# Gated linear attention with a routed spline layer on one core: a new order of the four engines in the loop, and the product into the output issued in two parts

## What is computed

```python
shift = silu(causal_depthwise_conv(x, conv_w, conv_b))      # 4 taps
r, k = split(shift @ in_proj_w.T)                            # 64 + 64
u = sigmoid(x @ ch_gate_w0.T @ ch_gate_w1.T + ch_gate_b1) * x
mg = shift @ mem_gate_w.T + mem_gate_b
sel = softplus(mg[..., :M]); tau = sigmoid(mg[..., M:])
g = -sel * tau
k = k / maximum(norm(k), 1e-12) * sel ** tau
def step(S, inp):                                            # over the tokens
    S = exp(g_t)[..., None] * S + k_t[..., None] * u_t[:, None, :]
    o_t = SCALE * einsum('bm,bmd->bd', r_t, S)
x = layernorm(x + o + shift * residual_weight)
# routed layer: signs of the normed x against the tiles' signatures give a
# cluster and a tile in it; 16 features of the token go through that tile's
# splines, scaled by each tile's minimum and maximum over all tokens
x = layernorm(x + x + out)
```

## Time and profile before

| what | value |
|---|---|
| three runs, us | 1296.23, 1296.49, 1297.90 |
| median, us | 1296.49 |
| the profiled execution, us | 1294.74 |
| its span, us | 1293.0 |
| PE busy | 1154.4 us, 89% |
| DVE busy | 1091.9 us, 84% |
| ACT busy | 952.5 us, 74% |
| POOL busy | 830.0 us, 64% |
| HBM read, written | 69.06 MB, 101.01 MB |

### The profile page before, as it was taken

One profiled execution on the slowest core, in us unless ns is written; L12 is line 12 of the kernel. 1 busy time (PEld: TensorE's weight loads), 2 busy tenths in 40 slices (PEclk: granted clock), 3 DMA queues, 4 the chain that ended last, 5 costly groups with the idle time before them and its releaser, 6 DMA issues. The chain is left out here.

```text
span 1293.0 us, 31770 instructions
## 1 busy us (share of the span) xinstructions
PE 1154.4 (89%) x9346; PEld 733.4 (57%) x9346; DVE 1091.9 (84%) x2532; ACT 952.5 (74%) x1809; POOL 830.0 (64%) x1669
## 2 busy tenths in 40 slices
PE   5799999999999999999999999999999977469730
PEld 4556666666666666666666666666666643333100
DVE  4898888898999899989898999899989883686885
ACT  4657888888888888888888888888888754514781
POOL 3125666777767676767676767676767664524486
PEclk8999999999999999999999999999999987655555
DMA  4012222222222222222222222222222115769998
GB/s 143 33 38 103 104 104 105 104 103 103 103 103 103 103 103 103 103 103 103 103 103 103 103 103 103 103 103 103 103 103 103 71 71 201 264 244 342 376 415 323
DMA packets 63347, 174.86 MB, mean 135 GB/s; under 512 B 11195, under 2 KB 22339, under 8 KB 63302
## 3 DMA queue, kind: packets, MB, share of 16 engines
q1 hardware_dynamic: 52646, 151.43, 31.5%
q10 hardware_dynamic: 5280, 20.97, 4.1%
q0 software_dynamic: 5376, 1.91, 1.0%
HBM read 69.06 MB, written 101.01 MB: 132 GB/s over the span
## 5 line engine op out<-in xcount | busy, mean ns | idle before, releaser
L1052 DVE SCALAR_TENSOR_TENSOR acc<-xT_all,cw_sb,acc 128x256 f32<-128x256 f32 x768 | 353.8, 518 | 6.8 <-ACT acc L751 6.8
L777 ACT ACTIVATE sg<-TX,bet,gam 128x256 f16<-128x256 f32 x256 | 129.8, 557 | 39.9 <-issue 20.1
L1384 POOL TENSOR_TENSOR AT<-AT,Wm 128x128 f32<-128x128 f32 x224 | 114.9, 513 | 40.6 <-DVE AT L1078 24.8
L484 PE MATMUL PR<-xT_all,w_sb 128*128 128x256 f32 x512 | 136.4, 390 | 4.2 <-ACT xT_all L715 4.2
L496 PE MATMUL WK<-w_sb,tS 128*128 128x512 f32 x256 | 137.3, 618 | 0.0
L751 ACT ACTIVATE acc<-xT_all,cb_sb,cw_sb 128x256 f32<-128x256 f32 x256 | 132.5, 592 | 4.8 <-DVE xT_all L1038 2.8
L538 PE MATMUL OB<-th_all,AT 128*128 128x512 f32 x256 | 124.6, 609 | 12.3 <-POOL AT L1384 10.7
L566 PE MATMUL PR<-shT,w_mg_sb 128*64 128x128 f32 x2048 | 128.9, 280 | 6.4 <-ACT shT L760 6.4
L566 PE MATMUL PR<-shT,w_rk_sb 128*64 128x128 f32 x2048 | 125.9, 276 | 0.0
L566 PEld LDWEIGHTS PR<-shT,w_rk_sb 128*64 128x64 f32 x2048 | 110.5, 137 | 25.7 <-issue 25.7
L566 PEld LDWEIGHTS PR<-shT,w_mg_sb 128*64 128x64 f32 x2048 | 113.5, 139 | 18.8 <-issue 12.0
(11 more groups left out here) (236 smaller groups left out, 2698.4 us busy)
## 6 DMA issues: line engine op xcount, KB each, us to landing
xin_all<-in_x SPq DMA_DIRECT2D x32, 1024.0 KB
y_ring<-y_all SPq DMA_DIRECT2D x32, 1024.0 KB, 4.1
y_scratch<-y_all SPq DMA_DIRECT2D x32, 1024.0 KB, 6.1
own<-y_scratch SPq DMA_DIRECT2D x5, 2048.0 KB, 16.3
rows<-y_scratch SPq DMA_DIRECT2D x4, 2048.0 KB, 12.5
out<-rows ACTq DMA_DIRECT2D x3, 2048.0 KB, 8.5
out<-own ACTq DMA_DIRECT2D x3, 2048.0 KB, 16.5
RX<-RE SPq DMA_DIRECT2D x128, 32.2 KB
```

Of the source, the lines that this page charges most:

```text
L484: i = pe.matmul(PR[:, 0:T], w0_sb[:, blk, :], xT[b][:, blk, HIST:HIST + T], start=(blk == 0), stop=(blk == NB - 1))
L777: nc.scalar.activation(sg[:, blk, :], TX[:, (blk % 2) * T:(blk % 2 + 1) * T], ACT.Sign, scale=gam[:, blk:blk + 1], bias=bet[:, blk:blk + 1 ...
L1052: v.scalar_tensor_tensor(acc[:, blk, :], xT[b][:, blk, i:i + T], cw_sb[:, blk, i:i + 1], acc[:, blk, :], ALU.mult, ALU.add).then_inc(e_con ...
L1384: q.tensor_tensor(late, late, Wm[:, :, l, :].rearrange("p c (n h) -> p c n h", h=h), ALU.add)\
```

## The change

It does four things.

- `output(c)` is split into `out_products(c)` (AT times th, and the transposes of zT) and `out_reads(c)` (RX times S). For chunk 0 the products go first and start the accumulation; for chunk 1 the reads go first, with an event of their own, e_r1, and the products follow later.
- On TensorE the projections w_mg and w_rk of a half stand side by side, so that there are two visits of the 128\*64 tiling where there were four; both come behind all four gate products, and the scores directly behind the second. Most other pieces change their place too.
- On ACT silu(0) and tap0(1) change their step, tanh(2), silu(1) and tanh(3) stand between y_out(1) and squares(1), and key_scale and level_exp follow squares(1) behind the table load.
- On DVE the three multiplications and normed(0) come at the end of the step, behind both gates; conv_round(0, 2) and (0, 3) pass to the next step. On GpSimd the same pieces start with mean(1), and differences now stands directly ahead of it; SP issues store, load, spread.

```diff
-            e_o, e_su, e_S, e_y = evs("e_o", 2), evs("e_su", 2), evs("e_S", 2), evs("e_y", 2)
+            e_o, e_su, e_S, e_y, e_r1 = evs("e_o", 2), evs("e_su", 2), evs("e_S", 2), evs("e_y", 2), ev("e_r1")
...
-                def output(c, k, b):
+                def out_products(c, k, b):
 
                     done(pe, e_res[1], k)
+                    done(pe, e_AT, k)
+                    wait(pe, e_u[c], k)
+                    for h in range(2):
+                        pe.matmul(OB[:, half_cols(h)], AT[:, c, :], th[b][c][:, half_cols(h)], start=(c == 0), stop=False)
+                    for blk in range(NB):
+                        i = pe.matmul(OB[:, blk * P:(blk + 1) * P], zT[b][:, blk, chunk_cols(c)], ident[:],
+                                      is_transpose=True, start=False, stop=(c == 1 and blk % 4 == 3))
+                    if c == 1:
+                        i.then_inc(e_o[c].sem, 1)
+
+                def out_reads(c, k, b):
+
                     pe.wait_ge(d_rx, (k + 1) * 64)
                     if c == 0:
                         earlier(pe, e_S[1], k, 1)
                     else:
                         wait(pe, e_S[0], k)
-                    done(pe, e_AT, k)
-                    wait(pe, e_u[c], k)
-                    for h in range(2):
-                        pe.matmul(OB[:, half_cols(h)], AT[:, c, :], th[b][c][:, half_cols(h)], start=True, stop=False)
                     for h in range(2):
                         rows = chunk_rows(h)
-                        pe.matmul(OB[:, half_cols(h)], RX[rows, c, 0:CH], S[c][rows, :], start=False, stop=False)
-                    for blk in range(NB):
-                        i = pe.matmul(OB[:, blk * P:(blk + 1) * P], zT[b][:, blk, chunk_cols(c)], ident[:],
-                                      is_transpose=True, start=False, stop=(blk % 4 == 3))
-                    i.then_inc(e_o[c].sem, 1)
+                        i = pe.matmul(OB[:, half_cols(h)], RX[rows, c, 0:CH], S[c][rows, :], start=(c == 1), stop=(c == 0))
+                    i.then_inc(e_o[c].sem if c == 0 else e_r1.sem, 1)
...
@@ decay on DVE, and the same in chunk_decay
-                        earlier(dve, e_o[1], k, 1)
+                        earlier(dve, e_r1, k, 1)
...
@@ step of GpSimd
+                    if live(g, 2):
+                        mean(1, *of(2))
+                        statistics(*of(2))
+                    if live(g, 3):
+                        gather(*of(3))
+                    if live(g, 1):
+                        assemble(*of(1))
+                    if live(g, 2):
+                        statistics_kept(*of(2))
+                    if live(g, 3):
+                        collect(*of(3))
+                    if live(g, 1):
+                        mean(0, *of(1))
                     if live(g, 0):
                         differences(*of(0))
-                    if live(g, 1):
-                        mean(0, *of(1))
-                    if live(g, 2):
-                        statistics_kept(*of(2))
-                    if live(g, 1):
-                        mean(1, *of(1))
-                        statistics(*of(1))
-                    if live(g, 2):
-                        gather(*of(2))
-                    if live(g, 0):
-                        assemble(*of(0))
-                    if live(g, 2):
-                        collect(*of(2))
-
-                pipeline(pool, step, 2)
+
+                pipeline(pool, step, 3)
```

More of the change, by code:

```diff
@@ L428, in step @@
                         first_rows()
-                    if live(g, 3):
-                        store(*of(3))
-                pipeline(sp, step, 3, NG // 2 - 1)
+                pipeline(sp, step, 4, NG // 2 - 1)
                 done(sp, e_A, NG - 1)
@@ new lines, in step @@
+                    if live(g, 4):
+                        signs(3, *of(4))
+                    if live(g, 1):
+                        tanh(1, *of(1))
+                    if live(g, 3):
+                        squares(0, *of(3))
+                        y_out(1, *of(3))
+                    if live(g, 1):
+                        tanh(2, *of(1))
+                        silu(1, *of(1))
+                        tanh(3, *of(1))
+                    if live(g, 3):
+                        squares(1, *of(3))
@@ L907, in step @@
-                    if live(g, 4):
-                        signs(2, *of(4))
-                    if live(g, 2):
-                        level_exp(*of(2))
-                    tables(SILU_AND_TANH)
-                    if live(g, 1):
-                        silu(1, *of(1))
-                        tanh(0, *of(1))
-                    if live(g, 3):
-                        y_out(1, *of(3))
-                        squares(0, *of(3))
-                    if live(g, 4):
-                        signs(3, *of(4))
```

232 lines of the change are left out of this document (118 added, 114 removed).

## The result

The changed kernel takes 1343.36 us (median of 4 runs, 1342.28 to 1344.08) against 1297.20 for the kernel before on the same chip: ratio 1.0365, 95% interval 1.0347 to 1.0384, 46 us slower. I had forecast 1300. The steady step, by t_blocks at 475.43 and 510.01, is 34.6 us instead of 32.38.

The account below looks back on a forecast made before the run. TensorE and the loop through GpSimd's AT, both 32.38 us a step, were taken to bound the kernel together. +10.9 (26 steps of +0.42), -6 and -1.5 at the ends gave 1298.1 on the profiled run, forecast 1300, range 1271 to 1312.

Parts of the forecast that it names:

- The sum of the loop: Loop from output products through four engines and GpSimd's AT: 32.80 us a step forecast, +0.42; bounds 31.8 and 33.6.
- +10.9, -6 and -1.5: Forecast parts in us: 26 steps of the longer loop, gain in the first steps, gain in the drain.
- AT, the loop that I named: Output products wait for the matrix AT that GpSimd assembles; TensorE was to idle about 1.1 us a step ahead of out_products(0).
- New waits: Passage of the forecast on waits the new order adds: e_r1 in decay and "e_cp" in collect, each priced at nothing.
- TensorE's sum: TensorE's own work in a step: fewer tiling visits were to save 0.70 us, giving 31.68 a step.
- Statistics to gather: GpSimd's stretch from first statistic to first gather: 6.76 us before, 7.41 forecast because VectorE holds it longer (+0.65).
- the holds I had put at 2.8 us: GpSimd locked out during the statistics by VectorE: 2.1 to 2.3 us by KE and RE, 0.6 by gate(1); 2.05 before.
- my reading of the 2.93 us row: A GpSimd copy ending with RE's multiply was read as GpSimd locked out through KE and RE, not let in between.
- TensorE stays the only bound: Rival: the loop finds slack and only TensorE's -0.70 a step counts; 1272 us, chance 0.14.
- Half of it: Rival: GpSimd gets in between KE and RE, holds stay 2.05, step -0.23; 1285 us, chance 0.19.
- A longer loop: Rival: mean(1) and squares(1) come late, step 33.05, 1306 us; with yn late too, up to 1316; chance 0.31.
- theory S: Formed during the experiments, not in the prediction: late TensorE signals take the gathers and the four RX transfers together.

Follow-up runs that it names:

- e17: Changed kernel without the four RX transfers of each group after the first (plain increment instead, stale values read): 1293.57 us, ratio 0.9975, step 32.75.
- e8: Kernel before with only the projections of a half put side by side: 1369.3 us, ratio 1.0558, step 34.7.
- e18: Changed kernel without the four gathers and with nothing long in their place (two small writes): 1270.03 us, ratio 0.9805, step 32.33.
- e5: Changed kernel with normed(1) directly behind normed(0) on VectorE: 1316.71 us, ratio 1.0194, steps of 34.5 to 36.9 and of 31.93 alternating.
- e13: Changed kernel with chunk_decay behind masked(1), so the RX transfers start later; normed(1) not moved: 1313.95 us, ratio 1.015, mean step 33.7.
- e11: Kernel of e5 with chunk_decay behind masked(1), so the RX transfers start later: 1289.96 us, ratio 0.9956, step 32.66.
- e2: Kernel before with the gathers replaced by GpSimd operations of about their length: 1283.62 us, ratio 0.9914, step 32.38.
- e1: Changed kernel with the gathers replaced by GpSimd operations of about their length: 1313.54 us, ratio 1.0141, step 33.7.
- e10: Kernel of e5 with the gathers replaced by GpSimd work of about the same length: 1310.62 us, ratio 1.011, step 33.8.
- e9: Kernel of e5 without the four RX transfers of each group after the first (plain increment instead, stale values read): 1288.19 us, ratio 0.9938, step 32.65.
- e6: Changed kernel with fill(2) and k_turned ahead of scores, and keT_out ahead of norm_log: 1379.23 us, ratio 1.066, step 35.5.
- e7: Changed kernel with the edits of e5 and e6 together: 1322.19 us, ratio 1.0214, steps of 35.25 and 31.99.
- e14: Kernel of e7 with chunk_decay behind masked(1): 1308.63 us, ratio 1.0107, steps of 34.6 and 32.02.
- e15: Kernel of e5 with two of the four RX transfers left out after the first group: 1325.37 us, ratio 1.0234, steps of 35.0 to 36.7 and 31.91.
- e16: Kernel of e11 with the second pair of gathers issued behind assemble on GpSimd: 1288.17 us, ratio 0.9949, step 32.64.
- e3: Changed kernel with assemble ahead of gather on GpSimd: 1391.51 us, ratio 1.0733, step 36.2.
- e4: Changed kernel with scores moved behind fill(2), squares_sum and t_blocks(0): 1350.04 us, ratio 1.042, step 34.8.
- e12: Kernel before with the split of the output alone, old order otherwise: 1296.07 us, ratio 0.9998, step 32.43.

## Why the prediction was wrong

- **The sum of the loop came near, in part by luck.** In e17, with the order as changed and no late signal, the step is 32.75; I had 32.80. Between first and last tS of the run e17 takes 6.0 us more than before, 2.6 less ahead of them and 4.4 less behind: -1.0 in span; I had +10.9, -6 and -1.5. But AT, the loop that I named, holds TensorE only in every second step there (6.4 us in 11 waits), and in the others yn does (4.4 in 12), a loop that I had as a rival; TensorE's idle time is 0.58 us a step where I had 1.1. Of the terms below, some are off by up to 0.5, with opposite signs. And I misread: the 10.7 us for AT in the kernel before are three waits, the longest 5.8, none of them between 240 and 1000 us, so they say nothing of the loop.
- **The step that failed: every wait for a result of TensorE was put at nothing behind the matmul's end.** Under "New waits" I priced only e_r1, at nothing, and TensorE's sum took its row distances over without idle time; k_turned to keT_out to states(0) had no term. Left out was the time from a matmul's end to the increment that its reader sees: in the changed kernel's trace 1.7 to 3.5 us where k_turned and the fill now stand, beside gathers and RX transfers, and TensorE sits 2.52 us a step for it. Before, k_turned ended 1.6 us ahead of the first gather. Set against e17's step, the late signals cost 34.6 - 32.75 = 1.85 us a step, and e17's ratio is 0.9975 where the changed kernel's is 1.0365: with signals on time there is no loss. What makes them late, and on which chips, stays open (below). A sign was there in the semaphore events of the kernel before: from 467.50 to 471.75, gathers and RX transfers running, only 5 increments of the engines are recorded, and a fill that ended at 471.27 has its own at 471.88. ScalarE came for it at 472.06, so it cost nothing.
- **Terms.** products(0) to products(1): 8.52 forecast, 8.53 measured. products(1) to y_out(1): 2.84, 2.79. To the first statistic: 4.75, 4.68. Statistics to gather: 7.41, 6.91; the holds I had put at 2.8 us are L1428, L1429 and L1422, 1.14 + 1.56 + 0.60, less the 0.19, 0.72 and 0.2 that such operations take alone, 2.19:

```profile
501.63 0.60 POOL L1422 TENSOR_TENSOR st<-ssm,consts 128x2 f32<-128x2 f32 x1 [1.90 <-ACT sq L776]
...
504.20 1.14 POOL L1428 TENSOR_TENSOR st<-st,consts 128x2 f32<-128x2 f32 x1
505.43 1.56 POOL L1429 TENSOR_TENSOR st<-st,minus_half 128x2 f32<-128x2 f32 x1
```

  L1428 ends at 505.34, KE's multiply at 504.07 + 1.23 = 505.30; L1429 ends 0.56 behind RE's (505.21 + 1.22 = 506.43). Each was held through one multiply, and one GpSimd operation got through where KE ended. That is what the Trainium skill's "SBUF — State Buffer", section "Who interferes with whom", says, and the statistics came 0.50 under my 7.41, as its rule would have it (I had put 0.3 to 0.5 on it). It is against my reading of the 2.93 us row; e8's 3.56 us, through nine instructions, is on the other side again. Both occur; what decides between them stays open. Gathers: 4.85, 5.07; assembly: 4.21, 4.34; TensorE's work in a step: 31.68, 31.96 in the changed kernel (34.58 less 2.62 idle), 31.9 in e18 and 32.2 in e17, so the new order gave TensorE 0.2 to 0.5 where I had 0.70.
- **Rivals.** "TensorE stays the only bound" is seen in e5's short steps alone. "Half of it" had GpSimd's holds right (2.19 where it had 2.05 and I 2.8), but not the time. "A longer loop", by mean(1) or late yn, pointed to the right side; yn did come late, but that is worth 0.36 us of waiting a step in e18, not the loss.
- **How far each run lies from the changed kernel.** From its 1.0365, by the ratios and 1297 us: normed(1) early -22 us (e5), RX transfers later -28 (e13), both -53 (e11), no RX transfers -51 (e17), no gathers -73 (e18; e2, with GpSimd as long as before, has 11 of that outside the loop). e5 and e13 were taken where signals come late; e11, e17 and e18 on chips where they come late in no trace, so their numbers hold the chip's part as well as the edit's, and the two can't be told apart.

**Open.** What makes the signals late is not shown. Read edit by edit, it looks as if the edits did it: none is late without gathers (e1, e10, e18) or without the RX transfers (e9, e17). Sorted by chip, the same traces say something else. The latest increment of TensorE (behind its matmul's end, 240 to 1000 us, some 500 increments each):

| chip | traces | latest, us |
|---|---|---|
| not on record | before, changed | 0.83, 3.63 |
| 12 | e5, e6, e7, e8 | 3.53, 4.23, 2.99, 1.17 |
| 1 | e13, e14, e15, e16 | 2.95, 2.74, 3.29, 1.56 |
| 8 | e1, e2, e3, e4 | 0.03 in each |
| 2 | e9, e10, e11, e12 | 0.03 in each |
| 10 | e17, e18 | 0.03 in each |

No chip has traces of both kinds, and on chips 8, 2 and 10 signals are on time in traces with all gathers and all RX transfers too (e3, e4, e11, e12). Two pairs set the same arrangement side by side. The first is e11 on chip 2 and e16 on chip 1: up to the end of k_turned the steps agree to 0.02 us, with two gathers begun 2.46 and 1.08 us ahead of it and no RX transfer yet. ScalarE's copy of the fill (L724), e11 and then e16:

```profile
456.00 0.41 ACT L826 ACTIVATE ge<-xa 128x256 f32<-128x256 f32 x1
456.98 0.60 ACT L724 ACTIVATE xT_all<-TX 128x512 f32<-128x512 f32 x1 [0.58 <-PE TX L455]
```

```profile
453.10 0.41 ACT L826 ACTIVATE ge<-xa 128x256 f32<-128x256 f32 x1
454.87 0.60 ACT L724 ACTIVATE xT_all<-TX 128x512 f32<-128x512 f32 x1 [1.36 <-PE TX L455]
```

The copy comes 0.79 us later in e16; its increment is 0.80 us late there and 0.01 in e11. All 36 increments of e16 that are over 0.5 us late come more than 28 us behind the last RX transfer. The second pair is the kernel before and e12 (chip 2), with gathers and RX transfers in the same places to 0.1 us: the fill that ends at 471.27 has its increment 0.61 us later, the one of e12, at 471.34, 0.01 later; in the 4.25 us from 1.68 behind the first gather the one trace holds 5 increments of the engines, the other 20.

So theory S is not the cause: the RX transfers are not needed (e14, e16), and gathers and transfers together are not enough (e4, e12). For the gathers speaks that every late increment comes within 3.3 us of the start of one; but no kernel without gathers was run on a chip with late signals. Where signals can come late, the arrangement does matter (e5's two kinds of step). The rival that fits all twenty traces is that the chip, or something in the state of that round, decides whether signals can be late at all. The run that would test it, the changed kernel itself on chip 8, 2 or 10, was not made. If it holds, the changed kernel would take about e17's time there, an estimate of 1290 to 1297 us by that run's range, and the forecast of 1300 would have been near on those chips.

The silence isn't TensorE's alone: in the changed kernel the trace holds 4 increments of all engines from 510.25 to 514.50, and in e17 19 in the same stretch behind its first gather (458.50 to 462.75), with each gather's 16 in one group. But some signals pass in such a silence without a record: in the kernel before the signs (L777) start at 468.85, 0.04 behind the y_turned for which they wait. So part of the silence is lost records and part is real delay, and whether the recording itself adds to the delay can't be told, since each time here is of a recorded execution.

## What to carry to other kernels

A wait that the order alone prices at nothing may still bound the loop, because a signal can come microseconds behind the work that it stands for. A wait put down to "remote" beside an idle engine is the sign to look for. Before work is moved, list for each new pair of producer and reader what DMAs are issued around the producer's end.

And when a series of runs is to name a cause, take the kernel that shows the effect once more in each round. Here each round had the kernel before beside it, which agrees within 0.3% on all chips, but not the changed one; so eighteen runs could not part the edit from the chip.

## What the runs showed of the hardware

- TensorE's increments came up to 4.2 us (e6; 3.6 in the changed kernel) behind the modelled end of their matmul, each of the late ones within 3.3 us of the start of an indirect gather on GpSimd; elsewhere mostly 0.01 to 0.03.
- This occurred in each of ten traces, those of the kernel before, of the changed kernel and of chips 12 and 1, and in none of ten on chips 8, 2 and 10 (latest 0.03 us), six of which have gathers.
- Four transfers of 32 KB each on SP's queue (RX) were not needed for it (e14: up to 2.5 us late with none issued for 30 us).
- A tiny GpSimd operation was held for 3.56 us through nine VectorE instructions with two SBUF inputs (e8), and elsewhere let in between two of them (1.14, then 1.56).
- Two-input work on GpSimd is no neutral stand-in for gathers of the same length: it stretched four VectorE instructions from 1.66 to 2.73 us (e10).
